# A fused embedding, rotation, expert and attention kernel: 64 composed pairs of steps in place of 56, matrices stored by pair, channel and parity, and work moved between GpSimd, ScalarE and TensorE

## The reference, cut to what matters

```
xn    = layernorm(h)
biv   = xn @ W_biv.T + b_biv        # 8 x 192 x 64 groups of 3
decay = sigmoid(xn @ W_decay.T + b_decay)
inj   = xn @ W_in.T + b_in
def step(s, (b_t, d_t, u_t)):       # s: 64 vectors of 3 for each batch entry
    s = d_t * rodrigues(b_t, s) + u_t   # rotate s by axis*angle b_t
states = scan(step, 0, ...)
h = h + states
h = h + experts(layernorm(h))       # 8 experts, best 2, gelu
h = h + linear_attention(layernorm(h))
h = h + experts(layernorm(h))       # 8 experts, best 2, silu
```

## Time and profile before

| | us |
|---|---|
| median of three runs (446.88 to 447.78) | 447.18 |
| the profiled execution: span from its first to its last instruction | 445.0 |
| what lies around the span, by the median | 2.2 |
| PE busy in the span | 412.3 (93%) |
| DVE busy | 289.9 (65%) |
| ACT busy | 230.6 (52%) |
| POOL busy | 219.3 (49%) |

### The profile page before, as it was taken

One profiled execution on the slowest core, in us unless ns is written; L12 is line 12 of the kernel. 1 busy time (PEld: TensorE's weight loads), 2 busy tenths in 40 slices (PEclk: granted clock), 3 DMA queues, 4 the chain that ended last, 5 costly groups with the idle time before them and its releaser, 6 DMA issues.

```text
span 445.0 us, 10881 instructions
## 1 busy us (share of the span) xinstructions
PE 412.3 (93%) x3803; PEld 302.7 (68%) x3803; DVE 289.9 (65%) x1351; ACT 230.6 (52%) x427; POOL 219.3 (49%) x260
## 2 busy tenths in 40 slices
PE   8999998988779999999889989968999999999993
PEld 5653655636534666666634569735999999999993
DVE  6689999999874444444487338996565565655651
ACT  1387945541755555555135113654666665665650
POOL 5302798699035677774400001335556666576534
PEclk9899799999989999999889999997999999999998
DMA  8709300010142122221299992094233333333313
GB/s 231 109 19 247 89 0 3 1 36 1 43 123 72 55 72 73 73 73 46 73 293 238 234 243 92 1 182 127 49 60 48 63 52 57 63 53 56 52 21 35
DMA packets 39892, 38.50 MB, mean 87 GB/s; under 512 B 7503, under 2 KB 37115, under 8 KB 39839
## 3 DMA queue, kind: packets, MB, share of 16 engines
q1 hardware_dynamic: 28909, 23.07, 22.1%
q0 software_dynamic: 9024, 13.44, 15.4%
q10 hardware_dynamic: 1906, 1.30, 1.0%
HBM read 27.73 MB, written 10.76 MB: 86 GB/s over the span
## 4 chain that ended last, share of the span: by engine, by line
PE 27%; DMA 11%; DVE 7%; issue 3%; ACT 2%; POOL 1%; POOLq 1%; ACTq 0%; DVEq 0%
PE bank L2034 9%; PE bank L2073 8%; DMA out<-a,idx 8%; DMA a<-expert_rows 2%; PE bank L2313 1%; PE bank L1879 1%; DVE h L1706 1%; PE bank L2422 1%; DVE st L1220 1%; PE bank L2004 1%; PE bank L2345 1%; PE bank L2319 1%; PE bank L2394 1%; ACT reg L1024 1%; PE bank L2367 1%
## 5 line engine op out<-in xcount | busy, mean ns | idle before, releaser
L769 POOL DMA_INDIRECT out<-a,idx x31 | 50.6, 1632 | 46.5 <-DMA out<-a,idx 32.5
L749 POOL DMA_INDIRECT reg<-xn_rows,idxs x59 | 57.6, 977 | 28.8 <-issue 16.2
L2034 PE MATMUL bank<-reg,xT 64*128 64x128 f32 x1116 | 69.0, 275 | 0.9 <-DVE reg L1623 0.9
L2034 PEld LDWEIGHTS bank<-reg,xT 64*128 64x128 f32 x1116 | 65.0, 188 | 1.1 <-DVE reg L1623 1.1
L2073 PE MATMUL bank<-reg 64*128 64x192 f32 x744 | 65.4, 323 | 0.0
L2073 PEld LDWEIGHTS bank<-reg 64*128 64x128 f32 x744 | 59.8, 187 | 0.0
L1879 PE MATMUL bank<-con 128*128 128x512 bf16 x201 | 55.2, 434 | 0.0
L1056 ACT ACTIVATE reg<-reg 128x1152 f32 x31 | 36.1, 1163 | 33.8 <-PE bank L2073 33.8
L1650 DVE TENSOR_SCALAR a<-bank,gs 128x192 f32<-128x192 f32 x31 | 13.0, 418 | 53.3 <-PE bank L2073 53.3
L1879 PEld LDWEIGHTS bank<-con 128*128 128x128 bf16 x201 | 21.6, 111 | 27.7 <-issue 12.1
L757 POOL DMA_INDIRECT expert_rows<-a,idx x28 | 27.6, 986 | 22.2 <-DVE a L1647 21.9
(11 more groups left out here) (373 smaller groups left out, 880.9 us busy)
## 6 DMA issues: line engine op xcount, KB each, us to landing
reg<-in_w2b SPq DMA_DIRECT2D x8, 576.0 KB, 8.6
reg<-in_w1b SPq DMA_DIRECT2D x8, 288.0 KB, 8.5
reg<-in_w1a SPq DMA_DIRECT2D x8, 216.0 KB
reg<-in_w2a SPq DMA_DIRECT2D x8, 216.0 KB
xn_rows<-xn SPq DMA_DIRECT2D x4, 384.0 KB, 2.7
reg<-in_w1b SPq DMA_DIRECT2D x8, 192.0 KB, 5.6
xn_rows<-xn SPq DMA_DIRECT2D x1, 1152.0 KB, 7.0
out<-h SPq DMA_DIRECT2D x1, 1152.0 KB
```

The source lines that it names most:

```text
L749: pool.indirect_dma_start(xs[:, i % RING, 0:(D, D2)[l]], None, xd[l], bass.IndirectOffsetOnAxis(ap=idxs[:, i:i + 1], axis=0)).then_inc(xs_ ...
L769: pool.indirect_dma_start(out, bass.IndirectOffsetOnAxis(ap=idx2[:, i:i + 1], axis=0), ys[:, i % YRING, :], None, compute_op=ALU.add).then ...
L2034: ins = MM(bank[2 + 2 * p + a][:, c * P:(c + 1) * P], w1r[rs, p, col:col + hc], xT64[rs, p, k, :], start=(c == 0 and k == 0), stop=(c == n ...
```

## The change

- `PBLK` is 8 blocks of 8, so `PAIRS` is 64 and `PAIR0`, the first token done by pairs, is 64 in place of 80. VectorE does 64 tokens singly and 64 pairs. GpSimd's share of the odd states is 49 pairs in pieces of 16, 16 and 17, VectorE's stays 15.
- `Mt` is stored as [pair, channel, parity, row, column]. So `biv`, `dec`, the projections' PSUM tiles and every tile of the chunk have the order (pair, channel, parity); a projection reads its moving operand in this order. The two matrices of a pair, over pairs and channels, are one dimension of stride 24.
- GpSimd's products of a block are 3 instructions of 128 x 384 in place of 9 of 128 x 128.
- The last group of text norms is written by GpSimd (`xnp_ready`), not by ScalarE.
- ScalarE's order: the last two transposes are copied out before the cosine of chunk 0; the squares of chunk 1 no longer wait for `m_ready`; text injections and roots come later; the second chunk's turns and the squares of the first's vectors come before the logits' copies; `trig_of(2)` comes between the diagonal and the other entries of chunk 1; `keep_pairs` and `keep_states` follow a new order.
- VectorE's reciprocals stand at steps 12 and 30. The patches' states are added after two blocks of pairs, not one.
- TensorE: `keep_busy(12, 6)` has 2 matmuls, `keep_busy(24, 1)` has 4. The h and basis matmuls (L2261) wait for all pair blocks. `pair_sums(1)` goes ahead of the patches' states.

The core of the diff:

```diff
-PBLK = (8,) * 7
+PBLK = (8,) * 8
-        Mt = mraw.rearrange("p (t a r c) -> p t a r c", a=NCH, r=3, c=4)
-        Mf = mraw.rearrange("p (t a e) -> p e a t", a=NCH, e=12)
+        Mt = mraw.rearrange("p (i a u r c) -> p i u a r c", a=NCH, u=2, r=3, c=4)
+        Mf = mraw.rearrange("p (q e) -> p e q", e=12)
+        Mp = mraw.rearrange("p (n u e) -> p u n e", u=2, e=12)
-        ODD = (0, 8, 24, 41)
+        ODD = (0, 16, 32, 49)
-        RECIP_AT = 18
+        RECIP_AT = (12, 30)
+        def matrix(t):
+            return Mt[:, t // 2, t % 2]
...
+            pool.wait_ge(rstd_ready, ln_sem(1, 2))
+            for j in GROUPS[1][2]:
+                G.tensor_scalar(xn[:, j, :], h[:, j, :], rstd[:, j:j + 1], nmr[:, j:j + 1], ALU.mult,
+                                ALU.add).then_inc(xnp_ready, 1)
...
                 for k in range(3):
-                    for r in range(3):
-                        ins = nc.gpsimd.tensor_tensor(term[b % 2][k][:, 0:n, :, r, :],
-                                                      second[:, :, :, r, k:k + 1].to_broadcast([P, n, NCH, 4]),
-                                                      first[:, :, :, k, :], ALU.mult)
-                    ins.then_inc(term_ready, 1)
+                    every = [P, n * NCH, 3, 4]
+                    nc.gpsimd.tensor_tensor(term[b % 2][k][:, 0:n].rearrange("p i a r c -> p (i a) r c"),
+                                            second[:, :, :, k:k + 1].to_broadcast(every),
+                                            first[:, :, k:k + 1, :].to_broadcast(every),
+                                            ALU.mult).then_inc(term_ready, 1)
...
-            steps(0, RECIP_AT)
+            steps(0, RECIP_AT[0])
             recip_of(dve, V, link, 1)
+            steps(RECIP_AT[0], RECIP_AT[1] - RECIP_AT[0])
             recip_of(dve, V, link, 2)
-            steps(RECIP_AT, TCH - RECIP_AT)
+            steps(RECIP_AT[1], TCH - RECIP_AT[1])
             dve.wait_ge(m_ready, 2)
             dve.wait_ge(ev_act, 8)
-            steps(TCH, PAIR0 - TCH)
             pair_steps(0)
+            pair_steps(1)
...
-                        ins = MM(ps[64 * hf:64 * hf + 64, :], wst[0:r, k, cc, w:w + 64],
-                                 xT[0:r, k, first + n * hf:first + n * hf + n], start=(k == 0), stop=(k == NK - 1))
+                        ins = MM(ps[64 * hf:64 * hf + 64, :].rearrange("p (i a u) -> p i a u", a=NCH, u=2),
+                                 wst[0:r, k, cc, w:w + 64],
+                                 xT[0:r, k, first + n * hf:first + n * hf + n].rearrange("p (a i u) -> p i a u", a=NCH, u=2),
+                                 start=(k == 0), stop=(k == NK - 1))
...
-            keep_busy(12, 6)
+            keep_busy(2, 6)
             t_pair(1, 4)
             t_pair(1, 5)
...
-            keep_busy(24, 1)
+            keep_busy(4, 1)
             pe.wait_ge(ev_act, 8)
...
             assemble(1)
             assemble(2)
+            pair_sums(1)
             pe.wait_ge(pair_ready, 1)
             patches_back()
-            pair_sums(1)
+            pair_sums(2)
+            pair_sums(3)
             t_pair(2, 0)
             t_pair(2, 1)
...
-            pe.wait_ge(pair_ready, 5)
+            pe.wait_ge(pair_ready, len(PBLK))
```

More of the change, by code:

```diff
@@ L276, in build @@
         comp = [of_pairs(a1f, sum(PBLK[:b]), n) for b, n in enumerate(PBLK[:6])]
-        comp += [of_pairs(setA.v.rearrange("p c a t -> p (c a t)"), 0, PBLK[6])]
-        PAIR_BANK = (0, 6, 7, 4, 5, 6, 7)
-        dodd = of_pairs(setA.trig.rearrange("p c a t -> p (c a t)"), 0, PAIRS - NODD)
+        comp += [of_pairs(setA.v.rearrange("p c q -> p (c q)"), sum(PBLK[6:b]), PBLK[b]) for b in (6, 7)]
+        PAIR_BANK = (0, 6, 7, 4, 5, 6, 7, 4)
+        dodd = of_pairs(setA.trig.rearrange("p c q -> p (c q)"), 0, PAIRS - NODD)
         assert o <= NR1
@@ L685, in _ @@
             pool.wait_ge(ev_act, 5)
-            late = dec[:, :, NPATCH:T]
+            late = dec[:, U:]
             G.tensor_scalar(late, late, 1.0, 0.0, ALU.add, ALU.max).then_inc(twice_ready, 1)
@@ L709, in _ @@
                 i0 = PAIR0 + 2 * sum(PBLK[:b])
-                first, second = Mt[:, i0:i0 + 2 * n:2], Mt[:, i0 + 1:i0 + 2 * n:2]
+                at = slice(i0 // 2 * NCH, (i0 // 2 + n) * NCH)
+                first, second = (Mp[:, u, at].rearrange("p n (r c) -> p n r c", c=4) for u in range(2))
                 pool.wait_ge(m_ready, (i0 + 2 * n - 1) // TCH + 1)
@@ L1380, in steps @@
                     for half in range(2):
-                        product(t, Mt[:, t], t, half)
+                        product(t, matrix(t), t, half)
                     if t % SLOTS == 0 and t >= 2 * SLOTS:
@@ L1404, in _ @@
             ln_start(2, 0, h)
-            pair_steps(1)
+            pair_steps(2)
             ln_end(2, 0)
-            for b in range(2, len(PBLK)):
+            for b in range(3, len(PBLK)):
                 pair_steps(b)
@@ L1922, in t_pair @@
                 else:
-                    pe.wait_ge(xn_ready, (n - 1) * NJ + 2 * q + 2)
+                    if n == 1 and q >= 4:
+                        pe.wait_ge(xnp_ready, 2 * (q - 4) + 2)
+                    else:
+                        pe.wait_ge(xn_ready, (0 if n == 1 else 2 * NJ - 4) + 2 * q + 2)
                 if m + q >= 2:
@@ L2242, in _ @@
             assemble(2)
+            pair_sums(1)
             pe.wait_ge(pair_ready, 1)
             patches_back()
-            pair_sums(1)
+            pair_sums(2)
+            pair_sums(3)
             t_pair(2, 0)
             t_pair(2, 1)
-            for b in range(2, len(PBLK)):
+            for b in range(4, len(PBLK)):
                 pair_sums(b)
             pe.wait_ge(xT_ready, XT_BASE[2] + 2)
-            pe.wait_ge(pair_ready, 5)
+            pe.wait_ge(pair_ready, len(PBLK))
             pe.wait_ge(base_ready, 1)
```

111 lines of the change are left out of this document (54 added, 57 removed).

## The result

| | runs | median us | ratio to before |
|---|---|---|---|
| before, beside the changed kernel | 9 | 446.88 | 1 |
| changed kernel | 9 | 449.79 | 1.0057 [1.0037, 1.0076] |
| changed kernel, a second time | 12 | 449.94 | 1.0058 [1.0031, 1.0084] |

By the ratio the change costs 2.5 us (the medians lie 2.9 us apart). 445.2 had been forecast, and the range ended at 447.8. In the profiled execution the span is 446.8 us (445.0 before), the time 448.61.

What follows compares the result with a forecast made beforehand. VectorE was taken to bound the recurrence up to 108 us. Steps 3.4, first block -1.0, two waits -1.0, a wait gone 0.5, start 0.5, last wait 0.5, clock -1.0: 1.9 us gained, 445.2 us against 447.18; range 442.8 to 447.8.

Steps and rivals of the forecast that it cites:

- What bounds the kernel, the steps: VectorE sets the recurrence's pace up to 108 us; eight fewer steps at 0.43 us save 3.4 us.
- The text projections: TensorE: start at 31.75 in place of 33.93, and take 12.26 us, the new reading order costing nothing (factor 1.0).
- the rival of the strided read: TensorE's projections read slowly; at factor 1.3 VectorE ends 2 us later than before, 449.2 us; chance 0.14.
- The wide products: GpSimd's block terms: three products of 128 x 384 at 0.9 us each, 2.7 us a block in place of 3.75.
- The rival that they save nothing: GpSimd's wide products stay at 3.75 us a block, so GpSimd binds, 446.6 us; chance 0.11.
- The start: VectorE's first step comes 0.45 us earlier, at 40.3, as norms move to GpSimd, idle at 26.6.
- ScalarE and GpSimd, chunk 1: ScalarE's new order has trig done at 47.5 against 50.3; GpSimd's quaternion has its last product at 55.5.
- The first block: First block of pairs is copied at 73.95; VectorE, ready at 72.3, waits 1.65 us in place of 0.61.
- The clock before L2275: TensorE idles 5.0 us before L2275; a fallen clock costs up to 2.0 us, taken as 1.0.
- The sum: Whole kernel: gain of 1.9 us, or 2.0 with rounding; span 445.0 becomes 443.0, time 445.2.
- The clock costs more: Rival: clock returns 2 us later in chunk 1's assembly and halves all of L2275; about no gain, 447.0; chance 0.13.
- The clock costs nothing: Rival: no clock loss at chunk 1's assembly or L2275, + 1.2 + 1.0, 443.0 us; chance 0.19.

Runs made afterwards that it cites:

- With the clock held: Changed kernel with fillers inside the logits, between the assemblies of chunks 1 and 2, and 24 ahead of the state sums: 443.78 us, ratio 0.9932.
- the runs with 24 fillers at either place: Changed kernel with 24 fillers ahead of state sums L2288 (5 before): 445.44 us; or between logits and chunk 1's assembly (4 before): 450.51 us.
- the versions with fillers: Changed kernel with fillers in logits, between assemblies and ahead of state sums: 443.78 us; the same with 6 in place of 2 behind the logits: 443.08 us.

## Why the prediction was wrong, point by point

- **What bounds the kernel, the steps:** right. 64 steps and two pairs of reciprocals took 76.20 - 39.88 - 4.05 = 32.27 us (32.0 forecast); eight steps fewer are eight steps fewer.
- **The text projections:** right, 12.69 us for 12.26, a factor of 1.035. With it the rival of the strided read falls; the 1.58 of the earlier trace rows was the worse bound of the two. The Trainium skill (SBUF — State Buffer, section "Door 1: The DMA port swizzle", on cachelines) says that two accesses to a 16-byte line are enough for full bandwidth, by which the factor is 1.0. The trace agrees to 3.5%.
- **The wide products:** right, 902 ns, 2.7 us a block. The rival that they save nothing falls.
- **The start:** wrong, by 0.86 us. 0.45 us earlier was forecast; from L1250 to the first step it is 14.70 us for 14.29. The wait of 0.47 us for the cosine's square went, as forecast. The step that failed is that GpSimd is free at 26.6 and costs nobody anything: three rows of VectorE beside its norms take 0.56 us more, and VectorE's writes of the entries a little more each (L1341 0.64 us, 0.60 in the trace of before; 0.64 too in the run without GpSimd's norms, so that part is the new layout).
- **ScalarE and GpSimd, chunk 1:** wrong in one instruction. The squares freed from their wait send L497 into VectorE's writes: 2.48 us in place of 0.73, and ScalarE's root behind it waits 1.00 us. The diagonal's time looks met, 56.45 forecast and 56.51 measured, but that is luck: this run began 1.3 us earlier than the one forecast from. Counted from L1250 the trigonometry was done after 47.73 - 25.18 = 22.55 us, forecast 47.5 - 26.48 = 21.02, and the diagonal after 31.33, forecast 29.97. The clock was forecast to be back 27.2 us after L1250 and was back after 28.6 (53.8). With the clock held the diagonal came after 56.54 - 26.64 = 29.90.
- **The first block:** the step that failed. 1.65 us of wait were forecast, 4.05 came. I priced the clock for the first assembly alone, there 1.4 us too early, and took for granted that the second runs at full speed since a wait of 1.75 us before 69.92 had left the clock up. Here 2.32 us before 63.95 did not: its first two sums took 3.85 us, 2.1 at full speed. Counted from L1250 the block came 3.55 us later than forecast (51.02 us, forecast 47.47): 1.5 were there when the second assembly started (38.77, forecast 37.27), and from its start to the block's sums it took 73.04 - 63.95 = 9.09 us for 7.39 before. VectorE itself came 1.15 us later than forecast (46.97, forecast 45.82), which leaves the 2.4. In the runs with 24 fillers at either place the same 2.32 us did leave the clock up, and in the one ahead of the state sums the code up to there is the changed kernel's: neither the length of the wait nor the code before it decides by itself, and what does is open. With the clock held the wait was 1.08.
- **The clock before L2275:** the mechanism right, the size wrong. It was bounded by 2.0 us and taken at 1.0; it was 5.82 - 3.18 = 2.64, as nearly the whole of the sums ran slowly and not part of them.
- **The sum.** 0.86 + (4.05 - 1.65) + (2.64 - 1.0) = 4.9 us; 0.2 more for the steps, and some 0.7 back: 4.4, which is the distance from -1.95 to +2.47. What came back is not in smaller waits (block 1 waited 0.27 for 0.5) but in the stretch behind VectorE's odd states: L1441 and L1444 took 0.65 and 0.37 us before, beside GpSimd's odd states, which ended at 111.21; as L1452 and L1455 they take 0.18 and 0.19, with GpSimd done at 105.89 + 0.56 = 106.45. That GpSimd is the cause there is not shown by a run.
- **The rivals.** "The clock costs more" was the one that came true, but its price, 2.0 - 1.2 - 1.0, had 1.2 us for the first assembly, 2.0 in all for L2288 (2.64 came) and nothing for the second assembly. It had the mechanism and stopped at no gain. "The clock costs nothing" gave 443.0; the versions with fillers measured 443.78 and 443.08.

The Trainium skill (GPSIMD Engine Reference, section "8. Key points") says that GpSimd shares its SBUF interfaces with VectorE and contends with VectorE's instructions "in a 2-port perf mode or with two SBUF inputs". The rows agree for L497: at 2.48 us it lies beside VectorE's writes, which read two SBUF operands, and it is 0.72 beside VectorE's steps, whose products read one operand from PSUM. L1316, which has one tile as input, took 0.49 us for 0.29 beside the norms; which case it is no run shows. I had not weighed it for instructions that only moved into a stretch in which VectorE is busy.

## What to carry to other kernels

Where a change makes one engine wait, ask what TensorE's clock does in that wait, and price the whole group of matmuls behind it at 1.8 times the row's duration (5.82 us for 3.18, 3.85 for 2.1); a bound between "none" and "part" was too low. Fillers belong between small matmuls and in the waits, not behind them in a heap: there they bring the clock back and push the work out by as much. And an instruction that is moved earlier meets other neighbours: look at what GpSimd and VectorE do at the same time before its duration is taken from the old row.

## What was not expected of the hardware

- A GpSimd tensor-tensor of 128 x 256 takes 0.72 us beside VectorE's steps and 2.48 us beside its writes; VectorE's instructions of 0.29 and 0.42 us take 0.49 and 0.61 beside GpSimd's norms. Not every one does: L547, a tensor-scalar at 27.30, took its 0.28 us while the norms ran on to 27.88.
- The same code ran its first assembly at 0.65 and at 1.00 granted clock in two kernels that differ only later; in another such pair the clock was down from 47.0 to 53.8 us and again from 64.0 to 67.5, or once from 46.8 to 57.0. The Trainium skill (TensorE: Matmul & The Clock Gate, section "What's actually happening") says that the throttled state is the default and activity releases it, and that at its start the same kernel gets a different number of slow matmuls from run to run. The profiles show the like in the middle of a kernel.
